# Four fused layers on one core: later weights converted later, base bias by tiles, output bias by accumulating transfers

## The chip, the cores and the metric

The kernel runs on one core of one Trainium2 chip. The metric is the device time in microseconds. TensorE multiplies, VectorE (DVE), ScalarE (ACT) and GpSimd (POOL) do elementwise work, and transfers are issued from the queues of SyncE (SP), GpSimd and, once, ScalarE. The engines run their own instruction lists in order and meet only in semaphores.

## The reference

Input x has 64 x 32 rows of 512 numbers, 2048 tokens in all, and there is a condition vector of 128 numbers for each of the 64 batches. Four layers follow one another, each with a residual:

```python
x = x + L0_ffn(L0_cond(x, cond))   # silu(c Wg^T) * (c Wu^T) Wd^T, width 1792
x = x + L1_ffn(L1_cond(x, cond))   # c W_base^T + b_base + top-2 of 8 LoRA experts of rank 16
x = x + L2_ffn(L2_cond(x, cond))   # c * sum(top-8 softmax of 64) + weights @ expert_bias
x = x + L3_ffn(L3_cond(x, cond))   # (c * in_scale) @ sign(W)^T * out_scale + bias
```

The conditioning step `cond` of layers 0, 2 and 3 mixes the 32 rows of a batch with a 32 x 32 matrix that a small network makes from the condition vector, and adds a bias; that of layer 1 is a grouped convolution over the 512 numbers with a bias. All is float32.

## The kernel before

The residual x lies in SBUF as `x_all`, 16 tiles of 128 tokens by 512. The work goes layer by layer, and in a layer over four groups `g` of four tiles (`GT` = 4, `G` = 4). Nothing is scheduled by a planner: each engine's list is written by hand, and the order in a list is the order in which it runs.

Layer 0 runs 14 slices of the feed-forward width for each group: gate and up products, silu on ScalarE, the product `hff` on VectorE, its high part on ScalarE and its low part `h_lo` on VectorE, and then the down product. `residual` (VectorE) adds the product to `x_all`. GpSimd's `part(g)` copies the new x of a group into a staging tile `prod`, which SyncE's `put_back(g)` writes to the DRAM scratch `y_dram`; SyncE's `regroup(g)` reads it back, shifted for the convolution, as 16 transfers into `stg`.

Layer 1, for each group: TensorE's `conv` makes the conditioned input from `stg`; VectorE's `cond1` turns it and adds `bias_bc` into `cT`; TensorE's `lora_a_router` makes the LoRA and router products, and `base` the base product of 32 matrix instructions. Meanwhile `route1` on VectorE shifts the logits, ScalarE takes their exponential (`exp`), and VectorE picks the two experts and writes `hm`. TensorE then runs the convolution of the next group, turns `hm`, and after ScalarE's copy `hmT` closes with `lora_b`. Base bias `bbase` is added to `x_all` by GpSimd's `base_bias(g)`, one instruction over four tiles, and VectorE's residual of the group waits for it (`s_base_bias`).

Between layers 0 and 1 ScalarE waits for the eight loads of the weights of layers 2 and 3 (`s_weights23`) and converts four of them: `eb_hi`, `in_w`, `out_w` and the signs `sgn` (`s_w_hi`). Only after these come its four exponentials. GpSimd makes the low halves of these weights after `base_bias(0)` and before `base_bias(1)`. SyncE issues the eight loads after `regroup(1)` and `bias(1, 1)`, and `put_back(3)` after them.

Layer 2 mixes with `cond`, routes with `route2`, and GpSimd's `add_scaled` adds the scaled input to `x_all`; VectorE's `final2` adds the rest (`s_x_new[2]`). In the last `layer2` TensorE runs `router3(0)`, waits for all of `s_x_new[2]`, and then for the chunks `FIRST3` of the mixing of group 1, with `turn_logits3(0)` after the first of them; `route3(0)` on VectorE needs that and follows `final2(3)` in VectorE's list.

Layer 3: ScalarE makes high halves (`high`) and copies the output scale (`out_scale`), VectorE and GpSimd make low halves, TensorE runs `sign_product`, VectorE rescales into `t1` (`s_rescaled`), GpSimd's `finish_3(g)` adds `t1` to `x_all`, and SyncE stores the tile. The output bias is added by GpSimd's `bias_3(g)`, four instructions, once the mixing has read the group.

Of the kernel before, what the change touches and what calls it, by code (L numbers as in the profile page):

```python
# [21 lines left out]
P = 128  # L22
D = 512
# [29 lines left out]
def build(nc, A, out):  # L53
    ctx = ExitStack()
    with ctx:
        def sb(name, shape, dt=F32):
            return ctx.enter_context(nc.sbuf_tensor(name, shape, dt))

        def sem(name):
            return ctx.enter_context(nc.semaphore(name))  # L60
# [82 lines left out]
        rb2 = sb("rb2", [P, E2])  # L143
        eb2 = sb("eb2", [P, D])
        wsg = sb("wsg", [P, S, D])
        bias3 = sb("bias3", [P, D])
        inc3 = sb("inc3", [P, D])
        outc3 = sb("outc3", [P, D])
        rcat = sb("rcat", [P, GT, P])
# [122 lines left out]
        s_scaled_hi = sem("s_scaled_hi")  # L272
        s_scaled_lo_even = sem("s_scaled_lo_even")
        s_scaled_lo_odd = sem("s_scaled_lo_odd")
        s_bias3 = sem("s_bias3")
        s_rescaled = sem("s_rescaled")
        s_tail = sem("s_tail")
        s_out = sem("s_out")
# [14 lines left out]
        def _(sp):  # L293
# [72 lines left out]
                sp.dma_start(dst[:], A[src]).then_inc(s_weights1, 16)  # L366
            regroup(1)
            bias(1, 1)
            sp.wait_ge(s_up, G * M)
            for dst, src in ((eb2, "eb2"), (inc3, "inc3"), (outc3, "outc3"), (wsg, "wsg"),  # L370
                             (wr2, "wr2"), (rb2, "rb2"), (wr3, "wr3"), (bias3, "bias3")):
                sp.dma_start(dst[:], A[src]).then_inc(s_weights23, 16)
            put_back(G - 1)
            for g in range(2, G):
                regroup(g)
                bias(1, g)
            for g in range(G):
                stage(g)
                bias(2, g)
# [12 lines left out]
        def _(pool):  # L392
# [73 lines left out]
            for g in range(1, G):  # L466
                block_diagonal(0, g)
                split_c(g)
                part(g - 1)
            block_diagonal(2, 0)  # L470
            part(G - 1)


            def base_bias(g):
                pool.wait_ge(s_weights1, LOADS1)
                xg = x_all[:, ds(g * GT, GT), :]
                pool.tensor_tensor(xg, xg, bbase[:].unsqueeze(1).broadcast_to([P, GT, D]),
                                   ALU.add).then_inc(s_base_bias, 1)

            pool.wait_ge(s_parted, NT)  # L480
            base_bias(0)
            pool.wait_ge(s_weights23, 16 * 8)
            pool.wait_ge(s_w_hi, 4)
            half = P // 2
            pool.wait_ge(s_base_bias, 1)
            pool.tensor_tensor(eb_lo[:], eb2[:], eb_hi[:].bitcast(F32), ALU.subtract).then_inc(s_w_lo, 1)
            pool.wait_ge(s_w_lo, 1)
            for n, (w, src) in enumerate(((in_w, inc3), (out_w, outc3))):
                pool.tensor_tensor(w[half:P], src[half:P], w[half:P].bitcast(F32), ALU.subtract).then_inc(s_w_lo, 1)
                pool.wait_ge(s_w_lo, n + 2)  # L490
            with pool.Fori(1, G) as g:
                base_bias(g)


            def add_scaled(g):
# [19 lines left out]

            def bias_3(g):
                pool.wait_ge(s_cond_mm[3], S * (g + 1))
                for j in range(g * GT, (g + 1) * GT):
                    pool.tensor_tensor(x_all[:, j, :], x_all[:, j, :], bias3[:], ALU.add).then_inc(s_bias3, 1)

            def finish_3(g, js):
                pool.wait_ge(s_bias3, GT * (g + 1))
                for j in js:
                    pool.wait_ge(s_rescaled, g * GT + j + 1)
                    xg = x_all[:, g * GT + j, :]
                    pool.tensor_tensor(xg, xg, t1[:, j], ALU.add).then_inc(s_x_new[3], 1)
# [19 lines left out]
        def _(pe):  # L546
# [155 lines left out]
            def layer1(g, more):  # L702
                base(g)
                pe.wait_ge(s_hm, g + 1)
                if more:
                    for q in range(Q - 1):
                        conv(g + 1, q)
                    pe.wait_ge(s_turned1, Q * (g + 1) + 1)
                    turn_hm(g)
                    conv(g + 1, Q - 1)  # L710
                    lora_b(g)
                    lora_a_router(g + 1)
                else:
                    cond(2, 0, SPARING, [nothing, nothing, nothing, lambda: (turn_hm(g), pe.wait_ge(s_cT[2], 1))])
                    lora_b(g)
                    pe.wait_ge(s_w_lo, 3)
                    pe.wait_ge(s_weights23, 16 * 8)
                    router2(0)
                pe.wait_ge(s_x_new[1], GT * (g + 1))


            def router2(g):
                pe.wait_ge(s_cT[2], S * (g + 1))
                for j in range(GT):
                    for s in range(S):
                        ins = mm(bank(4)[:, j * P:j * P + NPAD], cT[:, s, cols(j)], wr2[:, s], s == 0, s == S - 1)
                ins.then_inc(s_router2, 1)
# [7 lines left out]
            def layer2(g, more):  # L735
                for j in range(GT):
                    for s in range(S):
                        ins = pe.transpose(bank(j)[:, cols(s)], cT[:, s, cols(j)], ident)
                    ins.then_inc(s_c_back, 1)
                l, h = (2, g + 1) if more else (3, 0)  # L740
                cond(l, h, SPARING, [nothing, nothing, nothing,
                                      lambda: (turn_weights(g), pe.wait_ge(s_cT[l], S * h + 1))])
                pe.wait_ge(s_wT2, g + 1)
                for j in range(GT):
                    pe.wait_ge(s_t1, GT * g + j + 1)
                    mm(bank(j), wT[:, cols(j)], eb_hi[:], True, False)
                    mm(bank(j), wT[:, cols(j)], eb_lo[:], False, True).then_inc(s_product[2], 1)
                if more:
                    router2(g + 1)
                else:  # L750
                    pe.wait_ge(s_w_hi, 4)
                    router3(0)
                pe.wait_ge(s_x_new[2], GT * (g + 1))


            def router3(g):
# [91 lines left out]
        def _(act):  # L848
# [46 lines left out]
            layer0(G - 1, False)  # L895


            act.wait_ge(s_weights23, 16 * 8)
            act.wait_ge(s_product[0], G * GT)
            for dst, src in ((eb_hi, eb2), (in_w, inc3), (out_w, outc3)):  # L900
                copy(dst[:], src[:]).then_inc(s_w_hi, 1)
            act.activation(sgn[:], wsg[:], ACT.Sign).then_inc(s_w_hi, 1)

            def exp(s_ready, s_done, g, width):
                act.wait_ge(s_ready, g + 1)
                act.activation(ex[:, :, 0:width], lg[:, :, 0:width], ACT.Exp).then_inc(s_done, 1)

            with act.Fori(0, G) as g:
                exp(s_shifted1, s_exp1, g, E1)
                act.wait_ge(s_hm_turned, g + 1)  # L910
                copy(hmT[:], bank(4)).then_inc(s_hmT, 1)

            def scaled(g, j):
                act.wait_ge(s_c_back, GT * g + j + 1)
# [18 lines left out]
            for g in range(G):  # L933
# [11 lines left out]
                def out_scale(j):  # L945
                    act.wait_ge(s_out_scale, GT * g + j + 1)
                    copy(osc[:, j], bank(j)).then_inc(s_osc, 1)

                high(0)
                high(1)  # L950
                out_scale(0)
                high(2)
                high(3)
                for j in range(1, GT):
# [4 lines left out]
        def _(dve):  # L959
# [161 lines left out]
            with dve.Fori(0, G - 1) as g:  # L1121
                route1(g)
                cond1(g + 1)
                dve.wait_ge(s_base_bias, g + 1)
                residual(1, g)
            route1(G - 1)
            cond(2, 0, SPARING)
            dve.wait_ge(s_base_bias, G)
            residual(1, G - 1)


# [100 lines left out]
                    cond3(g + 1, [(s, UPPER[s]) for s in range(S)])  # L1232
            scale_out(G - 1, range(GT))

            dve.wait_ge(s_bias3, NT)
            dve.wait_ge(s_rescaled, NT)
            tt(x_all[:, NT - 1, D // 2:D], x_all[:, NT - 1, D // 2:D], t1[:, GT - 1, D // 2:D], ALU.add).then_inc(s_tail, 1)

# [89 lines left out]
```

## Time and profile before

| | |
|---|---|
| median of 3 runs (lowest, highest) | 588.41 us (588.16, 588.94) |
| the profiled execution | 588.53 us, of which the span is 586.3 us |
| busy: PE, PEld, DVE, ACT, POOL | 548.1, 420.5, 260.2, 133.9, 189.4 us |
| PE busy, tenths, slices of 14.7 us from 337.1 us | 9, 5, 2, 6, 9 |
| granted PE clock, tenths, same slices | 9, 8, 5, 8, 9 |
| chain that ended last | PE 80%, DVE 7%, issue 7%, DMA 2% |

"Busy" is the time in which an engine executed; PE is the matrix instruction itself and PEld its load of weights. The slices cut the span in 40. "Issue" in the chain is time in which an engine waited for nothing that the profile shows. A timeline row is: start in us, duration in us, engine, line, operation, target and sources, how many, and in brackets the idle time before with what ended it. Line 961 is a helper `tt` for VectorE, 548 the helper `mm` for TensorE and 850 the helper `copy` for ScalarE, so such rows are told apart by their tiles.

### The profile page before, as it was taken

Reading aid. Unit: us, or ns where it says so; the run is one execution under the profiler, and the core shown is the slowest. Engines: PE = TensorE matmul, PEld = TensorE weight load, DVE = VectorE, ACT = ScalarE, POOL = GpSimd, SP = SyncE. Lnnn points to the kernel's source line nnn. Section 1 sums busy time; section 2 is a strip of 40 time slices with the busy share of each in tenths; the row PEclk is TensorE's granted clock in tenths of the full one; section 3 lists DMA queues with packets and bytes.
Section 4 is the critical chain, followed back from the end, with each engine's and each line's share of the span. In section 5 each row is a group of like instructions: output and inputs, shape, how many; then the busy total and the mean of one; then the engine's idle time right before and its main releaser. Section 6 shows DMA issues by size and latency. Waiting matters only on the chain.

```text
span 586.3 us, 7216 instructions
## 1 busy us (share of the span) xinstructions
PE 548.1 (93%) x2689; PEld 420.5 (72%) x2689; DVE 260.2 (44%) x529; ACT 133.9 (23%) x230; POOL 189.4 (32%) x164
## 2 busy tenths in 40 slices
PE   7999999999999999999999995269999999989996
PEld 5788888888888888888888752035545589966884
DVE  4532245422227222253222340492526277887775
ACT  5322223222223222232222200310101022224332
POOL 2699981200004000012000000870000025478986
PEclk9999999999999999999999998589999999999999
DMA  8498130590001300003140099193681035111312
GB/s 298 152 421 305 29 91 0 123 181 0 0 0 55 106 0 0 0 1 89 27 101 1 0 121 237 48 120 41 81 151 18 14 111 137 28 19 18 126 70 111
DMA packets 84211, 50.32 MB, mean 86 GB/s; under 512 B 69600, under 2 KB 74464, under 8 KB 83424
## 3 DMA queue, kind: packets, MB, share of 16 engines
q1 hardware_dynamic: 82096, 38.97, 30.3%
q0 software_dynamic: 2016, 11.01, 5.2%
q8 instruction: 12, 0.20, 0.2%
q10 hardware_dynamic: 80, 0.08, 0.0%
q14 instruction: 7, 0.06, 0.0%
HBM read 31.93 MB, written 8.62 MB: 69 GB/s over the span
## 4 chain that ended last, share of the span: by engine, by line
PE 80%; DVE 7%; issue 7%; DMA 2%; POOL 1%; ACT 1%; SPq 0%; DVEq 0%; POOLq 0%
PE ps L548 80%; DMA xs<-in_x 2%; DVE cT L961 1%; POOL x_all L500 1%; DVE xs L961 1%; DVE c_lo L961 1%; DVE rest L1143 1%; DVE lg L961 1%; DVE t L961 0%; DVE c_lo_odd L961 0%; ACT c_hi L850 0%; DVE m L1139 0%; PE ps L732 0%; DVE rest L961 0%; PE ps L694 0%
## 5 line engine op out<-in xcount | busy, mean ns | idle before, releaser
L548 PE MATMUL ps<-c_lo,wl 128*128 128x512 f32 x448 | 173.0, 390 | 0.3 <-POOL c_lo L421 0.3
L548 PE MATMUL ps<-c_hi,wl 128*128 128x512 f32 x448 | 173.1, 390 | 0.2
L961 DVE TENSOR_TENSOR hff<-silu,ps 128x512 f32<-128x512 f32 x56 | 38.5, 688 | 164.5 <-PE ps L548 164.4
L548 PEld LDWEIGHTS ps<-c_lo,wl 128*128 128x128 f32 x448 | 84.1, 188 | 18.7 <-POOL c_lo L421 0.7
L548 PEld LDWEIGHTS ps<-c_hi,wl 128*128 128x128 f32 x448 | 84.1, 188 | 18.1 <-ACT c_hi L850 0.8
L548 PE MATMUL ps<-wl,h_hi 128*128 128x512 f32 x224 | 87.6, 391 | 0.0
L548 PE MATMUL ps<-wl,h_lo 128*128 128x512 f32 x224 | 87.2, 389 | 0.0
L961 DVE TENSOR_TENSOR h_lo<-hff,h_hi 128x512 fp32r<-128x512 f32 x56 | 44.8, 799 | 39.1 <-ACT h_hi L850 39.1
L421 POOL TENSOR_TENSOR c_lo<-cT,c_hi 128x512 fp32r<-128x512 f32 x8 | 10.7, 1342 | 157.7 <-ACT c_hi L850 157.7
L850 ACT ACTIVATE h_hi<-hff 128x512 fp32r<-128x512 f32 x56 | 35.4, 632 | 112.5 <-DVE hff L961 112.5
L884 ACT ACTIVATE silu<-ps 128x512 f32<-128x512 f32 x56 | 33.5, 598 | 116.4 <-PE ps L548 116.4
L548 PE MATMUL ps<-wbase,cT 128*128 128x512 f32 x128 | 55.6, 592 | 0.0
L548 PEld LDWEIGHTS ps<-wl,h_hi 128*128 128x128 f32 x224 | 42.0, 188 | 10.4 <-issue 1.7
L548 PEld LDWEIGHTS ps<-wl,h_lo 128*128 128x128 f32 x224 | 42.1, 188 | 8.5
L463 POOL COPY prod<-x_all 128x512 f32<-128x512 f32 x16 | 10.0, 642 | 111.7 <-DVE x_all L961 84.8
L548 PEld LDWEIGHTS ps<-wbase,cT 128*128 128x128 f32 x128 | 24.0, 190 | 28.7 <-issue 28.7
L548 PE MATMUL ps<-stg,wconv 128*64 128x512 f32 x64 | 18.6, 706 | 17.4 <-DVE hm L961 17.4
L961 DVE TENSOR_TENSOR cT<-ps,bias_bc 128x512 f32<-128x512 f32 x40 | 26.3, 686 | 19.2 <-PE ps L548 18.8
L433 POOL TENSOR_TENSOR blk<-agg,pack_c 128x512 f32<-128x512 f32 x9 | 9.4, 1041 | 75.7 <-PE ps L548 75.7
L548 PEld LDWEIGHTS ps<-blk,xs 128*128 128x128 f32 x256 | 31.3, 199 | 3.1 <-DMA xs<-in_x 1.9
L548 PE MATMUL ps<-blk,xs 128*128 128x128 f32 x256 | 32.4, 284 | 0.3 <-DMA xs<-in_x 0.3
L500 POOL TENSOR_TENSOR x_all<-x_all,t 128x512 f32 (+1 forms) x16 | 20.0, 1283 | 28.7 <-ACT t L915 28.7
(163 smaller groups left out, 649.9 us busy)
## 6 DMA issues: line engine op xcount, KB each, us to landing
wl<-in_wl POOLq DMA_DIRECT2D x14, 768.0 KB, 10.1
stg<-y_dram SPq DMA_DIRECT2D x64, 128.0 KB, 5.1
xs<-in_x SPq DMA_DIRECT2D x4, 1024.0 KB, 8.1
x_all<-in_x SPq DMA_DIRECT2D x1, 4096.0 KB, 14.7
y_dram<-prod SPq DMA_DIRECT2D x16, 256.0 KB, 2.2
xs<-x_all SPq DMA_DIRECT2D x4, 1024.0 KB, 4.9
out_x<-x_all SPq DMA_DIRECT2D x16, 256.0 KB, 2.0
bias_bc<-bias_dram SPq DMA_DIRECT2D x15, 256.0 KB, 5.3
```

The lines of the kernel that those rows point to most:

```text
L421: pool.tensor_tensor(c_lo[:, s], cT[:, s], c_hi[:, s].bitcast(F32), ALU.subtract).then_inc(s_c_lo_even, 1)
L433: pool.tensor_tensor(dst[:].rearrange("p j (b o) -> p j b o", b=TB), agg[:, COND[l], ds(g * GT, GT)].unsqueeze(2).broadcast_to([P, GT, TB, ...
L463: pool.tensor_copy(halves_x[:, j % 2], x_all[:, j, :].rearrange("p (s c h) -> p h s c", s=S, h=2)).then_inc(s_parted, 1)
L500: pool.tensor_tensor(xg, xg, t1[:, j:j + 1, :], ALU.add).then_inc(s_t1_added, 1)
L548: return pe.matmul(o, l, r, start=start, stop=stop)
L850: return act.activation(o, i, ACT.Copy)
L884: act.activation(silu[:, m % 2], bank(4 + 2 * (m % 2)), ACT.Silu).then_inc(s_silu, 1)
L961: return dve.tensor_tensor(o, a, b, op)
L1143: ins = dve.match_replace(rest[:, j], m8[:, j], logit[:, j], LOWEST)
```

## The change

On SyncE, `put_back(3)`, `regroup(2)` and `bias(1, 2)` go ahead of the loads of the later weights, which are seven, since `bias3` has no tile in SBUF any more; `regroup(3)` stays behind them. On ScalarE, the four conversions move from ahead of the exponentials into group 2, behind its `hmT` copy, and the loop over the groups is written out. On GpSimd, the base bias is added tile by tile, for groups 0 to 2 ahead of `part(3)` and for group 3 ahead of the low halves. On TensorE, the last `layer2` no longer waits for all of `s_x_new[2]`. On ScalarE, `out_scale(0)` of group 0 of layer 3 goes ahead of `high(0)`. On GpSimd, `bias_3(g)` issues one transfer that adds the bias from DRAM to the four tiles, with a semaphore for each group.

```diff
@@ SyncE
             regroup(1)
             bias(1, 1)
+            put_back(G - 1)
+            regroup(2)
+            bias(1, 2)
             sp.wait_ge(s_up, G * M)
             for dst, src in ((eb2, "eb2"), (inc3, "inc3"), (outc3, "outc3"), (wsg, "wsg"),
-                             (wr2, "wr2"), (rb2, "rb2"), (wr3, "wr3"), (bias3, "bias3")):
+                             (wr2, "wr2"), (rb2, "rb2"), (wr3, "wr3")):
                 sp.dma_start(dst[:], A[src]).then_inc(s_weights23, 16)
-            put_back(G - 1)
-            for g in range(2, G):
-                regroup(g)
-                bias(1, g)
+            regroup(3)
+            bias(1, 3)
@@ GpSimd
+            def base_bias(g):
+                for j in range(g * GT, (g + 1) * GT):
+                    pool.tensor_tensor(x_all[:, j, :], x_all[:, j, :], bbase[:], ALU.add).then_inc(s_base_bias, 1)
+
+            pool.wait_ge(s_weights1, LOADS1)
+            pool.wait_ge(s_parted, NT - GT)
+            for g in range(G - 1):
+                base_bias(g)
             block_diagonal(2, 0)
             part(G - 1)
...
             pool.wait_ge(s_parted, NT)
-            base_bias(0)
-            pool.wait_ge(s_weights23, 16 * 8)
+            base_bias(G - 1)
+            pool.wait_ge(s_weights23, 16 * 7)
             pool.wait_ge(s_w_hi, 4)
...
-            with pool.Fori(1, G) as g:
-                base_bias(g)
...
             def bias_3(g):
                 pool.wait_ge(s_cond_mm[3], S * (g + 1))
-                for j in range(g * GT, (g + 1) * GT):
-                    pool.tensor_tensor(x_all[:, j, :], x_all[:, j, :], bias3[:], ALU.add).then_inc(s_bias3, 1)
+                pool.dma_start(x_all[:, g * GT:(g + 1) * GT, :], A["bias3"].unsqueeze(1).broadcast_to([P, GT, D]),
+                               accum_op=ALU.add).then_inc(s_bias3[g], 16)

             def finish_3(g, js):
-                pool.wait_ge(s_bias3, GT * (g + 1))
+                pool.wait_ge(s_bias3[g], 16)
@@ TensorE, layer2
                 if more:
                     router2(g + 1)
+                    pe.wait_ge(s_x_new[2], GT * (g + 1))
                 else:
                     pe.wait_ge(s_w_hi, 4)
                     router3(0)
-                pe.wait_ge(s_x_new[2], GT * (g + 1))
@@ ScalarE
-            act.wait_ge(s_weights23, 16 * 8)
-            act.wait_ge(s_product[0], G * GT)
-            for dst, src in ((eb_hi, eb2), (in_w, inc3), (out_w, outc3)):
-                copy(dst[:], src[:]).then_inc(s_w_hi, 1)
-            act.activation(sgn[:], wsg[:], ACT.Sign).then_inc(s_w_hi, 1)
...
-            with act.Fori(0, G) as g:
+            for g in range(G):
                 exp(s_shifted1, s_exp1, g, E1)
                 act.wait_ge(s_hm_turned, g + 1)
                 copy(hmT[:], bank(4)).then_inc(s_hmT, 1)
+                if g == 2:
+                    act.wait_ge(s_weights23, 16 * 7)
+                    act.wait_ge(s_product[0], G * GT)
+                    for dst, src in ((eb_hi, eb2), (in_w, inc3), (out_w, outc3)):
+                        copy(dst[:], src[:]).then_inc(s_w_hi, 1)
+                    act.activation(sgn[:], wsg[:], ACT.Sign).then_inc(s_w_hi, 1)
...
+                if g == 0:
+                    out_scale(0)
                 high(0)
                 high(1)
-                out_scale(0)
+                if g > 0:
+                    out_scale(0)
```

VectorE's waits on `s_base_bias` count tiles, and its last wait on the output bias is for `s_bias3[3]`.

## Rows read from the trace of the kernel before

**Rows 1.** The page: the span.

```profile
span 586.3 us, 7216 instructions
```

**Rows 2.** The chain of waits, 340 to 416 us: start, us, what.

```profile
346.37 25.20 issue
```

**Rows 3.** Timeline of TensorE, 335 to 480 us.

```profile
345.75 13.90 PE L548 MATMUL ps<-wbase,cT 128*128 128x512 f32 x32
377.05 5.39 PE L548 MATMUL ps<-stg,wconv 128*64 128x512 f32 x12 [17.41 <-DVE hm L961]
...
415.75 1.12 PE L548 MATMUL ps<-stg,wconv 128*64 128x512 f32 x4
```

**Rows 4.** Timeline of ScalarE, 325 to 400 us.

```profile
366.52 0.63 ACT L850 ACTIVATE eb_hi<-eb 128x512 fp32r<-128x512 f32 x1 [31.10 <-DMA bias<-in_bias]
...
370.00 1.28 ACT L906 ACT_TABLE_LOAD   x1
```

**Rows 5.** Timeline of SyncE's queue, 325 to 475 us: the duration is that of issuing.

```profile
339.98 11.90 SPq L319 DMA_DIRECT2D stg<-y_dram  x16
...
352.67 3.37 SPq L372 DMA_DIRECT2D eb<-in_eb  x1
...
360.50 8.45 SPq L327 DMA_DIRECT2D y_dram<-prod  x4
```

**Rows 6.** Stages: length; PE, PEld, DVE, ACT, POOL busy (count); PEclk, DMA share, GB/s.

```profile
377.00:412.30 35.30, 29.80 (x92) 14.54 (x92) 18.66 (x35) 2.11 (x3) 14.66 (x4) 0.87 0.54 67
412.30:437.90 25.60, 25.60 (x95) 12.63 (x94) 10.75 (x35) 2.11 (x3) 0.00 (x0) 1.00 0.87 133
...
548.50:581.90 33.40, 32.65 (x210) 25.04 (x210) 22.37 (x45) 10.96 (x22) 28.89 (x22) 1.00 0.34 117
```

**Rows 7.** Timeline of VectorE, 335 to 415 us.

```profile
337.29 1.25 DVE L961 TENSOR_TENSOR cT<-tr,bias_bc 128x512 f32<-128x512 f32 x2
...
381.41 6.26 DVE L961 TENSOR_TENSOR cT<-tr,bias_bc 128x512 f32<-128x512 f32 x2
...
398.92 0.19 DVE L961 TENSOR_TENSOR lg<-ps,stat 128x32 f32<-128x32 f32 x1
...
401.76 0.69 DVE L961 TENSOR_TENSOR hm<-ps,lg 128x512 f32<-128x512 f32 x1
```

**Rows 8.** Timeline of GpSimd, 325 to 400 us.

```profile
344.27 1.22 POOL L463 COPY prod<-x_all 128x512 f32<-128x512 f32 x2 [73.94 <-DVE x_all L961]
...
377.68 14.34 POOL L477 TENSOR_TENSOR x_all<-x_all,bbase 128x2048 f32 x3 [0.37 <-POOL out_w L489]
```

**Rows 9.** Timelines of VectorE and of TensorE in layer 0, 290 to 297 us.

```profile
290.54 0.69 DVE L961 TENSOR_TENSOR hff<-silu,ps 128x512 f32<-128x512 f32 x1 [3.36 <-PE ps L548]
291.93 0.69 DVE L961 TENSOR_TENSOR h_lo<-hff,h_hi 128x512 fp32r<-128x512 f32 x1 [0.70 <-ACT h_hi L850]
...
295.71 0.39 PE L548 MATMUL ps<-wl,h_hi 128*128 128x512 f32 x1
```

**Rows 10.** Timeline of VectorE, 505 to 586 us.

```profile
521.50 0.75 DVE L1161 SCALAR_TENSOR_TENSOR x_all<-ps,stat,x_all 128x512 f32<-128x512 f32 x1 [0.48 <-POOL x_all L500]
523.61 0.19 DVE L1180 TENSOR_REDUCE stat<-ps 128x4 f32<-128x32 f32 x1 [1.36 <-PE ps L766]
```

**Rows 11.** Timeline of GpSimd, 505 to 586 us.

```profile
532.37 5.48 POOL L519 TENSOR_TENSOR x_all<-x_all,bias 128x512 f32<-128x512 f32 x4
...
562.13 5.02 POOL L519 TENSOR_TENSOR x_all<-x_all,bias 128x512 f32<-128x512 f32 x4
...
577.44 1.29 POOL L526 TENSOR_TENSOR x_all<-x_all,t 128x512 f32<-128x512 f32 x1 [0.28 <-DVE t L961]
```

**Rows 12.** GpSimd's loads of `wl` (durations in ns), and the page's transfers of `stg`.

```profile
L398 POOL DMA_DIRECT2D wl<-in_wl x14: 541/592/719, 4.6 to 28.0; - x14
...
DMA to landing us min/median/max: 4.5/10.1/18.1
...
stg<-y_dram SPq DMA_DIRECT2D x64, 128.0 KB, 5.1
```

More of the change, by code:

```diff
@@ L145, in build @@
         wsg = sb("wsg", [P, S, D])
-        bias3 = sb("bias3", [P, D])
         inc3 = sb("inc3", [P, D])
@@ L274, in build @@
         s_scaled_lo_odd = sem("s_scaled_lo_odd")
-        s_bias3 = sem("s_bias3")
+        s_bias3 = [sem(f"s_bias3_{g}") for g in range(G)]
         s_rescaled = sem("s_rescaled")
@@ L469, in _ @@
                 part(g - 1)
+            def base_bias(g):
[5 more added lines that the diff above has]
+                base_bias(g)
             block_diagonal(2, 0)
             part(G - 1)
[L474 to L478, printed above, removed]
             pool.wait_ge(s_parted, NT)
-            base_bias(0)
-            pool.wait_ge(s_weights23, 16 * 8)
+            base_bias(G - 1)
+            pool.wait_ge(s_weights23, 16 * 7)
             pool.wait_ge(s_w_hi, 4)
             half = P // 2
-            pool.wait_ge(s_base_bias, 1)
+            pool.wait_ge(s_base_bias, NT)
             pool.tensor_tensor(eb_lo[:], eb2[:], eb_hi[:].bitcast(F32), ALU.subtract).then_inc(s_w_lo, 1)
@@ L716, in layer1 @@
                     pe.wait_ge(s_w_lo, 3)
-                    pe.wait_ge(s_weights23, 16 * 8)
+                    pe.wait_ge(s_weights23, 16 * 7)
                     router2(0)
@@ L1123, in _ @@
                 cond1(g + 1)
-                dve.wait_ge(s_base_bias, g + 1)
+                dve.wait_ge(s_base_bias, GT * (g + 1))
                 residual(1, g)
@@ L1127, in _ @@
             cond(2, 0, SPARING)
-            dve.wait_ge(s_base_bias, G)
+            dve.wait_ge(s_base_bias, NT)
             residual(1, G - 1)
@@ L1233, in _ @@
             scale_out(G - 1, range(GT))
-            dve.wait_ge(s_bias3, NT)
+            dve.wait_ge(s_bias3[G - 1], 16)
             dve.wait_ge(s_rescaled, NT)
```

## The prediction

> **What bounds the kernel now.** I read the page's slices first (in the table above): TensorE is at nine tenths nearly everywhere, so only its holes can give anything. The one deep hole begins at 352 us. The profiled execution took 588.53 us, of which its span is 586.3 [rows 1]; the median of three runs is 588.41, so 0.1 us lower.
>
> The chain of waits names the hole. VectorE has the shifted router logits of group 0 of layer 1 ready at 346.4 and then stands for 25.20 us [rows 2]. In the timeline of TensorE the base product of group 0 runs from 345.75 to 359.6, and then comes nothing but an idle 17.41 us before the convolution of group 1 [rows 3]. ScalarE shows why: `eb_hi`, the first of four conversions of weights for layers 2 and 3, waits 31.10 us for the last load of the weights, and the exponential that VectorE needs is queued behind these four: it starts after its table load, 370.00 + 1.28 [rows 4]. The loads stand in SyncE's queue behind `regroup(1)`: 16 issues from 339.98 on, 11.90 us, then the eight loads from 352.67, then `put_back(3)` from 360.50 [rows 5].
>
> The hole has a tail. From 377.0 to 412.3 TensorE is busy 29.80 of 35.30 us at a granted clock of 0.87; the next, undisturbed round of the same work takes 25.60 us, all busy, at 1.00 [rows 6]. The 9.7 us of difference are 5.5 idle and 4.2 slow clock. The idle is VectorE's: two bias additions into `cT` take 6.26 us where the same pair takes 1.25 elsewhere [rows 7], and beside them GpSimd runs three base-bias additions of 2048 elements, 14.34 us together, 4.78 each [rows 8]. So a VectorE addition of two SBUF operands stood until one such GpSimd instruction ended.
>
> The Trainium skill, "SBUF — State Buffer", on contention, says the same: VectorE with two SBUF inputs and a GpSimd instruction that reads SBUF exclude each other for the whole instruction. By that rule an instruction cut to a quarter costs each VectorE addition at most a quarter of that wait.
>
> **The change part by part.**
>
> *The conversions behind exponential 2 (ScalarE), loads behind `regroup(2)` (SyncE).* Exponential 0 starts at about 346.6, its table loaded before. In an undisturbed round `hm` is written 3.5 us after the shift (398.92 to 402.45) [rows 7], so it is there at about 350, before the base product ends at 359.6. What is late next is `regroup(1)`: its last issue is at 351.9 [rows 5], and such a transfer takes 5.1 us to land [rows 12], so the data are there at about 357, before 359.6. Should they come later, each us costs one. The idle 17.41 us goes whole: -17.4. With no idle stretch ahead of it, the round of 35.3 us becomes one of 25.6: -9.7 more.
>
> SyncE's queue: `put_back(3)` now issues from 352.67. Its four issues, with the two copies of GpSimd between them, take 8.45 us now [rows 5], so GpSimd ends `part` at about 361 and `regroup(2)` waits for nothing but the convolution of group 1, done at about 364. It takes 11.9 us of issue [rows 5] and 5.1 to land, 17.0; the data are wanted 21.0 us after that convolution (its last part ends at 416.87 in the next round, which begins again at 412.3 + 25.6 [rows 3, 6]): no cost. The seven loads then issue from about 377. Now they take 366.5 - 352.7 = 13.8 us from the first issue to the conversion that waits for them [rows 4, 5], so they are there at about 391. ScalarE comes to them behind the transposed `hm` of group 2, at about 414: 23 us of cover, and `regroup(3)` cannot start before about 390 anyhow. The four conversions take 3.6 us (366.52 to the table load at 370.00 [rows 4]); the exponential of group 3 may come late by a few us without cost, because the base product of 13.9 us [rows 3] hides it. If that cover were gone it would cost 3.6 us.
>
> *Base bias by tiles.* Twelve additions (groups 0 to 2) move into layer 0, after the loads of `bbase`, which issue at the sixth slice of the last group, about 290.5 [rows 9]. GpSimd is idle there: its next row waits 73.94 us [rows 8]. Twelve at 1.28 us (that is 5.02 / 4 of an equal addition [rows 11]) make 15.4 us; even if those loads take 13.8 us, as the eight of layers 2 and 3 do, they end by 320. Beside them `h_lo` ends at 292.6 and its product is issued at 295.71, a slack of 3.1 us [rows 9], against one wait of 1.28, or 2.6 if both VectorE instructions of a slice wait: 0. The last four run at about 361 to 366, beside the first additions into `cT` of group 1. Bounds: 0, if the two miss each other; 2.6, if both additions of the first pair wait a whole instruction. I take +0.5, near the lower end, since an addition hits an instruction in mid-run and the additions are not the last thing TensorE waits for in an undisturbed round.
>
> *The wait dropped in the last `layer2`.* TensorE waits for all of group 3's new x, which ends at 522.25, though the first chunk of the mixing of group 1 reads only group 1 and writes a bank that is free. `turn_logits3` is queued behind this chunk, and VectorE starts `route3` at 523.61 [rows 10]. With the wait gone, chunk and transposition run while VectorE finishes; VectorE, whose order is unchanged, starts at 522.3. TensorE's own queue moves up as much. -1.3 us. The most it could fail by is all of it.
>
> *`out_scale(0)` first for group 0.* ScalarE's five copies keep their sum (0.63 us each [rows 4]), and the product waits for the last of the high halves, which stays where it is. 0, between -0.6 and +0.6.
>
> *The output bias by transfers.* GpSimd loses four additions of 5.0 us in each group [rows 11] and gets an issue instead: one of its issues takes 0.59 us [rows 12], and up to 5.0 it would cost no more than now. TensorE is busy 32.65 of the last 33.40 us before its end [rows 6], so GpSimd's freed time is worth 0 to 0.5; I take 0. What is new is that `finish_3(g)` waits for the landing. The tightest is the last: issued where the additions begin, 562.13, wanted by the first closing addition of group 3, 577.44 [rows 11]: 15.3 us. No accumulating transfer is in the trace. The nearest: loads of 768 KB from the same queue, 14 of them and most in each other's way, take 4.5 to 18.1, median 10.1 [rows 12]. Below 15.3 the cost is 0; at 18.1 it is 2.8. I take 10.1, the value of the same queue, so 0.
>
> The Trainium skill, "DMA: Bandwidth & Descriptors", on the software path, fits 2.0 us plus bytes over 436 GB/s, which would be an estimated 4.4 us for this size and no cost either; it has no figure for accumulating, and no row here shows one.
>
> **Sum.** 588.53 - 17.4 - 9.7 + 0.5 - 1.3 = 560.6.
>
> **The rivals.**
>
> *The transfers land late, but gain remains.* An accumulating transfer reads its target too, so it may be slower than the rows of plain loads. Between 15.3 and 20 us each us of landing adds one at the end, and above that up to two: 25 us give about 570. For it: no row shows this operation. Against it: the transfer queues are nearly empty in this stretch.
>
> *Slower than before: the same transfers as a chain.* `bias_3(3)` is issued after `finish_3(1)`, which waits for the landing of `bias_3(1)`, issued where its additions now start, 532.37 [rows 11]. With a landing time L the span is 532.4 + L + some 5 for the closing additions + L + 8.9 (from 577.44 to the end) - 27.8 for what is gained ahead = 518.5 + 2L. It decides from L = 34 us; at 40 it gives a span of 598.5, a time of about 601. That is twice the slowest landing seen.
>
> *The stall only moves.* Weights landing later than the end of ScalarE's `hmT` copy of group 2 would hold exponential 3. It takes over 23 us of delay before it starts to cost; or contention in layer 0 or round 1 is larger than the rows say (each VectorE instruction waits for more than one of the tile additions). Then the tail of 9.7 is not won: up to 570.
>
> **How the numbers follow.** Forecast 0.88: 560.6, own range 558.7 to 565.8. The low end takes away the 0.5 of contention, 0.5 for the freed GpSimd and 0.6 plus rounding for `out_scale`; the high end adds 2.1 of contention, 2.8 for landing and 0.3. Late landing with gain 0.06, tail not won 0.04, slower than before 0.02. A measurement of this kernel tells about 0.2% (1.2 us) from no change. Faster 0.97, same 0.01, slower 0.02. The range is the forecast's own.
>
> **What would show it.** Right: no idle TensorE between base product and convolution in the first round of layer 1, granted clock 1.00 there, rounds of 25.6 to 26.5 us; twelve base-bias rows on GpSimd between 295 and 320; `route3` of group 0 starting 0.1 us after the last new x; accumulating transfers landing in under 15 us. Wrong: an idle of VectorE or TensorE at `finish_3`, `hm` of group 0 later than 359 us, a `cT` addition in round 1 of over 2 us, or a slice of layer 0 longer than at present.

## The result and the profile after

The changed kernel takes 561.52 us (559.42 to 561.84, four runs) against 588.67 us (588.16 to 589.56, four runs): a ratio of 0.953, 95% interval 0.9503 to 0.9556. The profiled execution took 561.39 us, its span 559.6.

The page: span, busy slices of TensorE, granted clock.

```profile
span 559.6 us, 7186 instructions
PE   7999999999999999999999999999999999989996
PEclk9999999999999999999999999999999999999999
```

The hole is gone, and the granted clock is at nine tenths or more in every slice. The answer to [rows 3] is this timeline of TensorE: the base product ends where the convolution begins, and the router product of the next group waits for nothing.

```profile
346.96 13.90 PE L546 MATMUL ps<-wbase,cT 128*128 128x512 f32 x32
360.79 2.91 PE L546 MATMUL ps<-stg,wconv 128*64 128x512 f32 x12
...
368.84 3.97 PE L546 MATMUL ps<-war,cT 128*128 128x136 f32 x32
372.65 13.90 PE L546 MATMUL ps<-wbase,cT 128*128 128x512 f32 x32
386.47 2.91 PE L546 MATMUL ps<-stg,wconv 128*64 128x512 f32 x12
```

The exponential of group 0, which stood behind the conversions in [rows 4], now follows VectorE's shift at once:

```profile
347.61 0.23 ACT L898 ACTIVATE ex<-lg 128x32 f32<-128x32 f32 x1 [9.68 <-DVE lg L962]
```

GpSimd's timeline, against [rows 8]: twelve base-bias tiles run in layer 0, four beside the first round of layer 1.

```profile
301.54 16.49 POOL L472 TENSOR_TENSOR x_all<-x_all,bbase 128x512 f32<-128x512 f32 x12 [31.05 <-DMA wlb<-in_wlb]
...
360.43 5.40 POOL L472 TENSOR_TENSOR x_all<-x_all,bbase 128x512 f32<-128x512 f32 x4
```

VectorE's additions into `cT` in that round, against the 6.26 us of [rows 7]: 2.89 for the pair that meets GpSimd, 1.24 for the other.

```profile
363.49 2.89 DVE L962 TENSOR_TENSOR cT<-tr,bias_bc 128x512 f32<-128x512 f32 x2
...
367.54 1.24 DVE L962 TENSOR_TENSOR cT<-tr,bias_bc 128x512 f32<-128x512 f32 x2
```

**The ledger by stages.** TensorE's timeline repeats so exactly that starts of the same instruction cut the span into stages that can be compared between kernels (us). Each column is a difference of two starts: S0, from 0 to the router product of group 0; A, to the convolution of group 1; B, to that of group 2 (round 1); C, to that of group 3; D, to the last transposition of layer 2's weights; E, to the first mixing chunk of `FIRST3`; F, to `in_scales(0)`; H, to `router3(1)`; I, to the end of the span.

| kernel | S0 | A | B | C | D | E | F | H | I |
|---|---|---|---|---|---|---|---|---|---|
| before | 341.96 | 35.09 | 35.27 | 25.55 | 78.05 | 6.38 | 5.08 | 6.06 | 52.86 |
| changed | 343.18 | 17.61 | 25.68 | 25.55 | 78.03 | 5.03 | 5.07 | 6.66 | 52.79 |
| difference | +1.22 | -17.48 | -9.59 | 0 | 0 | -1.35 | 0 | +0.60 | -0.07 |

From the start of the router product on, the changed kernel is 27.92 us shorter. S0 is 1.22 us longer, and the chain of waits puts that into the first 20 us, ahead of everything that was changed: the load of the first x, and the small matrix instructions behind it. Changed kernel first, then the kernel before:

```profile
2.13 12.58 DMA xs<-in_x
...
14.75 4.65 PE ps L546 x20
```

```profile
2.13 12.12 DMA xs<-in_x
...
14.29 3.95 PE ps L548 x20
```

Over all runs below S0 lies anywhere from 340.77 to 343.18 us, with no order by kernel. So the medians scatter by some 2 us through the start alone, and where a few tenths matter I read the stages.

The 20 small instructions belong to the 32 of the first mixing. These in the changed kernel, then in e10 below, where S0 is 340.78:

```profile
14.75 5.99 PE L546 MATMUL ps<-blk,xs 128*128 128x128 f32 x32 [0.61 <-DMA xs<-in_x]
```

```profile
14.12 4.16 PE L545 MATMUL ps<-blk,xs 128*128 128x128 f32 x32
```

Within the 32, one starts every 0.21 us up to 19.3 us in the changed kernel, 17.4 in the one before and 15.0 in e10, and every 0.11 us from there on. In all fourteen profiles S0 less the end of these 32 is 322.3 to 322.5 us. So the scatter of S0 is the 0.8 us between their earliest and latest start and, for the larger part, the moment at which their rate doubles. The halved spacing fits TensorE's two clock levels of 1.2 and 2.4 GHz, but the profile gives a granted clock of 1.00 for this stretch, so the clock is inferred here, and no run shows why the moment differs.

### The profile page after: what moved, and what is told of

Same layout as the page of the kernel before. It is cut to its first block, busy times and chain, and to the rows that moved or that the text cites. A ratio compares the mean times of both kernels' runs of the same rounds, so it can differ in the third digit from the quotient of the medians.

```text
span 559.6 us, 7186 instructions
## 1 busy us (share of the span) xinstructions
PE 545.0 (97%) x2689; PEld 419.3 (75%) x2689; DVE 251.9 (45%) x529; ACT 129.9 (23%) x227; POOL 177.7 (32%) x164
## 4 chain that ended last, share of the span: by engine, by line
PE 91%; DVE 5%; DMA 2%; issue 1%; ACT 1%; SPq 0%; DVEq 0%
PE ps L546 89%; DMA xs<-in_x 2%; DVE c_lo L962 1%; DVE cT L962 1%; DVE t L962 0%; DVE rest L1144 0%; PE ps L692 0%; PE ps L730 0%; PE ps L786 0%; PE ps L736 0%; DVE wcat L962 0%; DVE c_lo_odd L962 0%; DVE m L1140 0%; DVE lg L962 0%; DVE rest L962 0%
## 5 line engine op out<-in xcount | busy, mean ns | idle before, releaser
L472 POOL TENSOR_TENSOR x_all<-x_all,bbase 128x512 f32<-128x512 f32 x16 | 21.9, 1403 | 31.1 <-DMA wlb<-in_wlb 31.1
L463 POOL COPY prod<-x_all 128x512 f32<-128x512 f32 x16 | 10.1, 644 | 54.8 <-DVE x_all L962 37.3
L1013 DVE STREAM_TRANSPOSE tr<-ps 128x512 f32<-128x512 f32 x16 | 11.2, 708 | 34.3 <-PE ps L546 34.3
```

The costliest lines, as they stand in the source:

```text
L463: pool.tensor_copy(halves_x[:, j % 2], x_all[:, j, :].rearrange("p (s c h) -> p h s c", s=S, h=2)).then_inc(s_parted, 1)
L472: pool.tensor_tensor(x_all[:, j, :], x_all[:, j, :], bbase[:], ALU.add).then_inc(s_base_bias, 1)
L1013: dve.transpose(tr[:, q % 2], bank(4 + q)).then_inc(s_turned1, 1)
```

## The experiments

**e1: the conversions alone.** The kernel before with this edit only:

```diff
-            act.wait_ge(s_weights23, 16 * 8)
-            act.wait_ge(s_product[0], G * GT)
-            for dst, src in ((eb_hi, eb2), (in_w, inc3), (out_w, outc3)):
-                copy(dst[:], src[:]).then_inc(s_w_hi, 1)
-            act.activation(sgn[:], wsg[:], ACT.Sign).then_inc(s_w_hi, 1)
...
-            with act.Fori(0, G) as g:
+            for g in range(G):
                 exp(s_shifted1, s_exp1, g, E1)
                 act.wait_ge(s_hm_turned, g + 1)
                 copy(hmT[:], bank(4)).then_inc(s_hmT, 1)
+                if g == 0:
+                    act.wait_ge(s_weights23, 16 * 8)
+                    act.wait_ge(s_product[0], G * GT)
+                    for dst, src in ((eb_hi, eb2), (in_w, inc3), (out_w, outc3)):
+                        copy(dst[:], src[:]).then_inc(s_w_hi, 1)
+                    act.activation(sgn[:], wsg[:], ACT.Sign).then_inc(s_w_hi, 1)
```

> The kernel before, with one edit: the four conversions move behind the hmT copy of group 0 (with group 2 the low halves on GpSimd would wait for ever, since base_bias(1) is queued behind them). My theory: the idle 17.4 us between base product and convolution goes, but put_back(3) still stands behind the eight loads, so base_bias(0) ends only at about 373, the residual of group 0 waits for it, and TensorE idles about 6 us in round 1: 588.5 - 17.4 - (9.7 - 7.5) = about 569 us (566 to 572). Rival (the conversions are the whole of it, the moves on SyncE and GpSimd are worth nothing): 561.5 us. Rival (the 9.7 us of tail is lost in full whatever ScalarE does): 571 us and a round 1 of over 35 us.

Measured: 568.17 us (567.79 to 569.77), ratio 0.9656 [0.9638, 0.9674]. Stage A is 17.61 us, as in the changed kernel, and B 31.86. TensorE's base product of group 1, and VectorE's residual of group 0 that released it:

```profile
375.88 15.67 PE L548 MATMUL ps<-wbase,cT 128*128 128x512 f32 x32 [4.17 <-DVE x_all L961]
```

```profile
372.89 2.48 DVE L961 TENSOR_TENSOR x_all<-x_all,ps 128x512 f32 x4 [6.58 <-POOL x_all L477]
```

The idle stretch belongs to ScalarE's order alone. What stays is the late base bias: VectorE stands 6.58 us for it, TensorE 4.17, and its clock falls to 0.89 in the 15.7 us behind. My theory stands.

**e2, e3, e4: size and place of the base bias.** In the changed kernel, e2 and e3 put all of it behind `part(3)`:

```diff
-            pool.wait_ge(s_weights1, LOADS1)
-            pool.wait_ge(s_parted, NT - GT)
-            for g in range(G - 1):
-                base_bias(g)
             block_diagonal(2, 0)
             part(G - 1)
+            pool.wait_ge(s_weights1, LOADS1)
             pool.wait_ge(s_parted, NT)
-            base_bias(G - 1)
+            for g in range(G):
+                base_bias(g)
```

e2 and e4 make it one instruction over four tiles, with the waits counted in groups:

```diff
-                for j in range(g * GT, (g + 1) * GT):
-                    pool.tensor_tensor(x_all[:, j, :], x_all[:, j, :], bbase[:], ALU.add).then_inc(s_base_bias, 1)
+                xg = x_all[:, g * GT:(g + 1) * GT, :]
+                pool.tensor_tensor(xg, xg, bbase[:].unsqueeze(1).broadcast_to([P, GT, D]),
+                                   ALU.add).then_inc(s_base_bias, 1)
```

> The changed kernel, with all four base-bias additions behind part(3), as before, and each one instruction over four tiles, as before. My theory: they run from about 360 to 380 beside the additions into cT of round 1; each of these waits for the end of one instruction of 4.8 us, so the pairs take 5 to 6 us again instead of 2.9 and 1.2 and TensorE idles 6 to 9 us: 567 to 571 us. Rival (the tail came from the cold clock behind the idle stretch, not from GpSimd): 561.5 us, since the idle stretch is gone here too.

> The changed kernel, with the sixteen base-bias additions by tiles, all behind part(3). My theory: the additions into cT wait for one instruction of 1.3 us each, 5 us in all less about 1.5 us of slack: 2.5 to 4 us over the changed kernel, 564 to 565.5 us. Rival (the size of the instruction doesn't matter, only the total of 20 us beside VectorE): the same time as with the coarse ones there. Rival (only the size matters, the place is worth nothing): 561.5 us.

> The changed kernel, with the base bias in its new places, but one instruction over four tiles. My theory: three instructions of 4.8 us beside layer 0, where the slack of h_lo is 3.1 us: each can hold a down product by up to 1.7 us, and the one of group 3 holds the first addition into cT by about 1.7 us: 0.5 to 5 us over the changed kernel, 562 to 566.5 us. Rival (layer 0 hides everything, whatever the size): 561.5 us, within 0.5.

Measured: e2 573.0 us (572.8 to 574.55), e3 562.17 (561.49 to 562.65), e4 559.79 (559.73 to 561.62). Stage B: 38.60, 28.28 and 25.55 us, against 25.68 in the changed kernel and 25.55 in an undisturbed round.

VectorE in e2, then TensorE in e2:

```profile
361.99 6.95 DVE L961 TENSOR_TENSOR cT<-tr,bias_bc 128x512 f32<-128x512 f32 x2
...
370.10 8.65 DVE L961 TENSOR_TENSOR cT<-tr,bias_bc 128x512 f32<-128x512 f32 x2
```

```profile
378.80 5.43 PE L545 MATMUL ps<-war,cT 128*128 128x136 f32 x32 [11.34 <-DVE cT L961]
```

VectorE in e3, then TensorE in e3:

```profile
361.98 3.31 DVE L960 TENSOR_TENSOR cT<-tr,bias_bc 128x512 f32<-128x512 f32 x2
...
366.44 3.42 DVE L960 TENSOR_TENSOR cT<-tr,bias_bc 128x512 f32<-128x512 f32 x2
```

```profile
369.92 3.97 PE L544 MATMUL ps<-war,cT 128*128 128x136 f32 x32 [2.46 <-DVE cT L960]
```

One VectorE addition loses up to one GpSimd instruction: 15.60 us for four additions beside instructions of 4.8 us, 6.73 beside those of 1.3, and 2.5 alone. e2 lies outside what I expected: I took the waits to be no more than in the kernel before. There the additions began beside the first of three instructions, the pair of [rows 7] lost 5.0 us and the next pair 3.1, and TensorE stood 5.5 us in the round [rows 6]. Here four instructions followed without a gap and TensorE stood 11.34 us; the granted clock was 0.76 over the 15 us up to 378.8 and 0.71 over the 5.2 us behind, so the router product took 5.43 us for 3.87.

The rival that put the whole tail down to the idle stretch ahead is out: there was none, and the tail was longer than ever. But a part of the tail is the idle stretch's, which I had not separated. Two stretches of the kernel before, in the columns of [rows 6], with the granted clock third from the end:

```profile
377.00:382.40 5.40, 5.35 (x13) 1.29 (x13) 2.34 (x3) 0.00 (x0) 5.03 (x3) 0.50 0.00 0
393.20:398.50 5.30, 5.27 (x33) 5.27 (x34) 2.37 (x4) 0.00 (x0) 0.00 (x0) 0.71 1.44 160
```

The first is the convolution right behind the 17.41 us of idle: at 0.50 it took 5.39 us [rows 3], and in e2, with no idle stretch ahead, 2.91. That, and 0.1 us in the transposition behind it, makes 2.6 us of the 9.7. The second is the router product behind VectorE's stall, 5.42 us for 3.87: with the 5.5 us of idle, some 7 us are GpSimd's.

e3 in its stage is 2.6 us over the changed kernel, as expected, though its median shows 0.7 of it, since its S0 was 1.5 us shorter.

e4 shows what I had not worked out: three instructions of 4.8 us beside layer 0 cost nothing. S0 alone could not show it, since it scatters by more. But behind the first 25 us the chain of waits is one run of 1449 matrix instructions up to the router product: 318.57 us in e4, 318.49 in e3, where nothing lies beside layer 0, 318.63 in the changed kernel and 318.56 in the one before. The timeline of GpSimd in e4:

```profile
300.43 14.69 POOL L472 TENSOR_TENSOR x_all<-x_all,bbase 128x2048 f32<-128x2048 f32 x3 [31.38 <-DMA wlb<-in_wlb]
```

So the place is what gains; the cut into tiles gains nothing in its new place. Whether some other timing of these three would hold a down product was not tried.

**e5: output bias by GpSimd's instructions.** The changed kernel with the old `bias_3` and `bias3` as an eighth load.

```diff
-                pool.dma_start(x_all[:, g * GT:(g + 1) * GT, :], A["bias3"].unsqueeze(1).broadcast_to([P, GT, D]),
-                               accum_op=ALU.add).then_inc(s_bias3[g], 16)
+                for j in range(g * GT, (g + 1) * GT):
+                    pool.tensor_tensor(x_all[:, j, :], x_all[:, j, :], bias3[:], ALU.add).then_inc(s_bias3[g], 1)
```

> The changed kernel, with the output bias added by GpSimd's instructions again (bias3 loaded as an eighth weight). My theory: the transfers land in 9.4 us where 15.3 are free, and GpSimd's time is not on the path, so neither form costs anything: 561.5 us, within 0.7, and the layer 3 stretch of the same length within 0.3. Rival (GpSimd's freed time is worth something): 562 to 563 us.

Measured: 560.06 us (558.13 to 561.66). Its stages from the router product to the end add up to 216.45 us, those of the changed kernel to 216.42; stage I is 52.94 against 52.79. That 0.15 us is too little to tell from one profile of each. My theory stands; the median is lower by the start (S0 341.95).

**e6: the wait back.**

```diff
                 if more:
                     router2(g + 1)
-                    pe.wait_ge(s_x_new[2], GT * (g + 1))
                 else:
                     pe.wait_ge(s_w_hi, 4)
                     router3(0)
+                pe.wait_ge(s_x_new[2], GT * (g + 1))
```

> The changed kernel, with TensorE's wait for all of the new x of group 3 back behind router3(0). My theory: route3(0) starts 1.3 us behind the last new x again: 562.8 us (562.4 to 563.2). Rival (the product of group 0 waits for the low halves anyway and the gain is lost there): 561.5 us.

Measured: 562.11 us (560.32 to 563.38); stage E 6.40 us against 5.03, all other stages within 0.05. The wait is worth 1.37 us and no other stage takes it back.

```profile
494.29 1.16 PE L546 MATMUL ps<-prod,x_all 128*128 128x128 f32 x8 [1.30 <-DVE x_all L1162]
```

**e7: the output scale behind the high halves.**

```diff
-                if g == 0:
-                    out_scale(0)
                 high(0)
                 high(1)
-                if g > 0:
-                    out_scale(0)
+                out_scale(0)
```

> The changed kernel, with out_scale(0) of group 0 behind high(0) and high(1) again. In the changed kernel the stretch from scale_in to the first rescaled product grew from 5.0 to 5.6 us, with VectorE's two low halves at 3.05 us where they took 2.3, so the early output scale holds the high halves 0.5 us and makes the low halves of VectorE and GpSimd collide. My theory: 560.9 us, 0.4 to 0.7 under the changed kernel. Rival (the collision comes from GpSimd's missing bias additions): 561.5 us with the same 5.6 us.

Measured: 559.47 us (558.92 to 561.45); stage H 6.07 us against 6.66. VectorE's low halves of group 0 in e7, and the chain of waits of the changed kernel over the same stretch:

```profile
501.31 0.86 DVE L959 TENSOR_TENSOR c_lo<-cT,c_hi 128x512 fp32r<-128x512 f32 x1
502.42 1.44 DVE L959 TENSOR_TENSOR c_lo<-cT,c_hi 128x512 fp32r<-128x512 f32 x1 [0.25 <-ACT c_hi L848]
```

```profile
501.61 0.60 ACT osc L848
502.21 1.05 ACT c_hi L848 x2
503.25 0.02 issue
503.28 3.06 DVE c_lo L962 x2
506.34 0.04 issue
506.38 2.63 PE ps L546 x37
```

The early copy costs 0.59 us, and e5 rules out the rival: with GpSimd's bias additions back, H was 6.65. What e7 gave back elsewhere is stage B, 26.23 us against 25.68: the four base-bias tiles met VectorE's additions at a worse moment. From the router product to the end e7 takes 216.33 us against 216.42, so nearly all of the 2.05 us between the medians is the start (S0 340.77). e1 and the kernel before, with their own order, have H at 6.06.

**e8, e9: landing made longer.** The changed kernel with one (e8) or two (e9) more accumulating transfers of 1 MB into a spare tile ahead of each bias transfer; each group's extra transfers wait for those of the group before. GpSimd also clears the spare tile once, behind the base bias.

```diff
+                pool.dma_start(spare[:], A["bias3"].unsqueeze(1).broadcast_to([P, GT, D]),
+                               accum_op=ALU.add).then_inc(s_spare, 16)
                 pool.dma_start(x_all[:, g * GT:(g + 1) * GT, :], A["bias3"].unsqueeze(1).broadcast_to([P, GT, D]),
                                accum_op=ALU.add).then_inc(s_bias3[g], 16)
```

> The changed kernel, with one more accumulating transfer of 1 MB into a spare tile issued ahead of each bias transfer on the same queue. The bias transfers landed in 9.1 to 9.7 us where 15.3 are free. My theory: landing of 15 to 18.8 us and so 0 to 3.5 us at the end: 561 to 565 us. Rival (queued transfers don't delay each other): landing under 11 us, 561.5 us. Rival (the issue itself, 1.3 us each on GpSimd, is what counts): 562.8 us and more with landing unchanged.

> The same with two more transfers ahead of each. My theory: landing of 21 to 28 us, which is beyond the 15.3 us free, so finish_3 waits and the end moves by 6 to 13 us: 567 to 575 us, with GpSimd idle ahead of its closing additions. Rival (there is more room than 15.3 us, since VectorE and TensorE need finish_3 only one group later): under 564 us.

Measured: e8 564.19 us (564.02 to 564.36, two runs), e9 580.14 (both runs). GpSimd's transfers into `x_all` in the changed kernel, in e8 and in e9 (least, median, most):

```profile
DMA to landing us min/median/max: 9.1/9.4/9.7
```

```profile
DMA to landing us min/median/max: 13.7/15.4/17.8
```

```profile
DMA to landing us min/median/max: 17.8/21.9/25.4
```

In e8 the time is as expected and the reason is another. `finish_3` waited 0.7 us in all, ahead of group 0. What ended last was SyncE's 256 KB load of the mixing bias of group 3, which VectorE needs for `cond3(3)`; the waits, and the chain:

```profile
DVE xs L972 <- DMA bias_bc<-bias_dram: 2.6, 1, 2.6
POOL x_all L534 <- DMA x_all<-in_bias: 0.7, 1, 0.7
```

```profile
520.17 15.08 DMA bias_bc<-bias_dram
```

Stage I grew by 4.2 us: TensorE stood 2.6 us for VectorE there, and the granted clock was 0.76 over the 7.2 us behind. The slowest such load takes 6.8 us in the kernel before, 9.3 in the changed one and 15.1 in e8, and where GpSimd adds the bias itself 5.9 (e5) and 6.8 (e12): the bias transfers of GpSimd's queue slow the small load of SyncE's. Both rivals of e8 are out, since landing did grow.

e9 came out far above its range, 19.5 us of it in stage I. This is no clean test: GpSimd stood 13.4 us for the experiment's own order between spare transfers.

```profile
POOL x_all L535 <- DMA x_all<-in_bias: 14.0, 3, 9.8
POOL spare L525 <- DMA spare<-in_bias: 13.4, 3, 4.6
```

The rival with more room is out all the same. The last bias transfer was issued at 547.30, and `finish_3(3)` stood for it at the very end of the chain:

```profile
571.24 3.94 POOL L535 TENSOR_TENSOR x_all<-x_all,t 128x512 f32<-128x512 f32 x3 [9.75 <-DMA x_all<-in_bias]
```

That is 23.9 us of landing, of which 14.2 were covered, near the 15.3 I had worked out. The 25.4 us are those of group 2.

**e10: SyncE's order as before.**

```diff
             bias(1, 1)
-            put_back(G - 1)
-            regroup(2)
-            bias(1, 2)
             sp.wait_ge(s_up, G * M)
...
-            regroup(3)
-            bias(1, 3)
+            put_back(G - 1)
+            for g in range(2, G):
+                regroup(g)
+                bias(1, g)
```

> The changed kernel, with SyncE's order as before: the seven loads ahead of put_back(3) and regroup(2). My theory: put_back(3) ends about 8 us later, regroup(2) is issued from about 371 and has landed at about 388 where TensorE wants it at 386.5: 0.5 to 2 us, 562 to 563.5 us. Rival (the loads' place is what removed the stall): 570 us or more. Rival (no cost, there is cover): 561.5 us.

Measured: 559.64 us (559.15 to 560.12); stage B 25.54 us. My theory falls and so does the rival that made the loads' place the cause: it costs nothing. SyncE's queue, and TensorE's convolution of group 2:

```profile
357.86 8.92 SPq L326 DMA_DIRECT2D y_dram<-prod  x4
366.89 10.85 SPq L318 DMA_DIRECT2D stg<-y_dram  x16
```

```profile
383.93 2.91 PE L545 MATMUL ps<-stg,wconv 128*64 128x512 f32 x12
```

`regroup(2)` begins at 366.9, 4 us earlier than I had put it, and is issued by 377.7. With the median landing of 5.1 us it is there at an estimated 382.8, 1.1 us ahead of its use. GpSimd's last four tiles moved behind VectorE's additions, so round 1 is even 0.14 us shorter.

**e11: the best of both.** The changed kernel with e7's and e4's edits.

> The changed kernel, with out_scale(0) of group 0 behind the high halves again and the base bias in its new places as one instruction for four tiles. The runs so far give 0.6 us for the first (the stretch from in_scales to router3(1) was 6.07 us against 6.66) and 0.1 us for the second (round 1 of 25.55 us against 25.68). My theory: 0.7 us under the changed kernel, 560.8 us, and both stretches as short as in the single runs. Rival (the two meet elsewhere): 561.5 us.

Measured: 558.86 us (558.1 to 559.22), ratio 0.948 [0.9466, 0.9495]. Stage H is 6.07, B 25.67; from the router product to the end 215.79 us against 216.42. Of the 2.7 us between the medians 0.6 are the edits, the rest is the start (S0 341.11). The 0.1 us of e4 did not come back: one instruction of 4.5 us met the first additions at another moment (pair of 2.87 us).

**e12: three edits alone.** The kernel before with the conversions behind group 2, the base bias by tiles in its new places and the dropped wait; all else as before.

> The kernel before with three of the edits alone: the conversions behind group 2, the base bias by tiles in its new places, and the dropped wait. SyncE's order, the output bias by GpSimd's instructions and the place of out_scale(0) are those of before. My theory: these three are the whole gain. Round 1 of 25.54 us as in the run with the loads ahead, 6.07 us from in_scales to router3(1) as in the run with out_scale behind, so 0.6 to 0.7 us under the changed kernel: 560.8 us or less, within 0.4% of it. Rival (the loads ahead and the additions on GpSimd meet and cost something together): 562 us and more, with a longer round 1 or a wait of TensorE in layer 3.

Measured: 560.05 us (559.55 to 560.25), ratio 0.9505 [0.9484, 0.9525]. The stages are 17.61, 25.55, 25.54, 78.02, 5.02, 5.07, 6.05 and 52.84: 215.70 us, the shortest of all fourteen profiles, and 28.6 under the kernel before. Three of the six edits are the whole gain.

| stage | before | e1 | e2 | e3 | e4 | e6 | e7 | e10 | e11 | e12 | changed |
|---|---|---|---|---|---|---|---|---|---|---|---|
| A | 35.09 | 17.61 | 17.61 | 17.61 | 17.61 | 17.61 | 17.61 | 17.61 | 17.60 | 17.61 | 17.61 |
| B | 35.27 | 31.86 | 38.60 | 28.28 | 25.55 | 25.63 | 26.23 | 25.54 | 25.67 | 25.55 | 25.68 |
| E | 6.38 | 6.41 | 5.03 | 5.03 | 5.03 | 6.40 | 5.04 | 5.02 | 5.03 | 5.02 | 5.03 |
| H | 6.06 | 6.06 | 6.66 | 6.67 | 6.66 | 6.66 | 6.07 | 6.66 | 6.07 | 6.05 | 6.66 |

## Why the prediction was right, term by term

The forecast of 560.6 us is 0.8 under the profiled execution of 561.39, and the changes come out as forecast in place and nearly in size. That the terms' 27.9 us meet the stages' 27.92 so closely is partly luck: contention came out 0.4 us cheaper than I took it, `out_scale(0)` 0.6 us dearer.

- *Idle stretch, -17.4.* Stage A: -17.48. e1 shows that ScalarE's order alone gives it. `regroup(1)` was in time, as worked out.
- *Tail, -9.7, with +0.5 for contention.* Stage B: -9.59, so contention cost 0.13. It was nearer to its lower end than I took it: one pair took 2.89 us instead of 1.25, but TensorE needs it only 1.5 us later. Three runs agree on these 1.5 us: the additions of the round lost 1.6 us here, 2.2 in e7 and 4.2 in e3, and the round grew by 0.13, 0.68 and 2.73. So the moment at which GpSimd's instructions meet them decides.
- *The cause of the tail.* I split it as 5.5 idle and 4.2 clock, and did not say whose the clock is. With no idle stretch ahead and GpSimd's instructions back, e2 has a tail with both parts. But of the 4.2 us 2.6 came from the idle stretch ahead, the convolution at a clock of 0.50, and only the rest from the stall that GpSimd caused. Both causes were removed, so the term was right as a whole.
- *Tiles.* I gave the gain to moving and cutting together. e4 shows that the cut is worth nothing once twelve tiles lie in layer 0; e3 shows that the cut alone would have left 2.6 us.
- *SyncE's order, 0.* Right for the changed kernel, but the edit is no condition of the gain either (e10). What I had not seen is that the old order has 1.1 us of cover.
- *Dropped wait, -1.3.* Stage E: -1.35; e6: 1.37.
- *`out_scale(0)` first, 0 within 0.6.* Stage H: +0.60, the upper bound. This is the step that failed, the point value and its reason. I argued that the product waits for the last high half, which stays where it is. It does, but behind it comes the last low half. The first two high halves moved 0.6 us later, GpSimd's two low halves then run without a gap, and VectorE's two, which exclude each other with them, take 3.05 us instead of 0.86 and 1.44 with a gap.
- *Output bias, 0.* Stage I: -0.07, e5 0.15. Landing was 9.4 us, close to the 10.1 I took, which is luck: that was the median of plain loads of another size, most of them in each other's way; an issue takes 1.3 us rather than 0.59, under the 5.0 it replaces. What the late-landing rival missed is another queue: at landings of 13.7 to 17.8 us (e8) `finish_3` hardly waited, but the load of `bias_bc` on SyncE's queue was late.
- *The start.* 1.2 us of S0 are in no term; no edit touches them, and they lie in the first mixing, as shown above.

The Trainium skill, "SBUF — State Buffer", on the pair of ports that VectorE and GpSimd share, says that the later one blocks for the whole instruction. e2 and e3 agree, with 3.3 and 1.1 us lost for each addition beside instructions of 4.8 and 1.3 us. The fit of the Trainium skill, "DMA: Bandwidth & Descriptors", on the software path, gave an estimated 4.4 us for a plain transfer of this size; the accumulating one took 9.4, and the measurement decides.

## What to carry to other kernels

When an engine stands for "issue", follow the queue of the engine that should release it: work of a later stage, parked at a stage boundary, held the first instruction of the next stage here, and moving it behind the first loop round (e1) gave 20.9 of the 27.9 us. Then look for what is late next, which here was another engine's long instruction excluding VectorE, and move that to a stage with slack before cutting it. Undo the parts one at a time: three of six edits carried everything, and one of the others cost 0.6 us.

## What the runs showed of the hardware that I had not expected

An accumulating transfer of 1 MB from DRAM, bias rows repeated four times, landed in 9.1 to 9.7 us alone and 15.4 behind another of its kind, so the second added 6.0; and such transfers slowed a 256 KB load of another queue, made of 128 B pieces, from at most 6.8 us to 9.3 and 15.1.

A TensorE stall of 11.34 us (e2) was followed by a router product of 5.43 us instead of 3.87, at a granted clock of 0.71, a mean over both levels of 1.2 and 2.4 GHz. One of 5.45 us (kernel before) cost the same, 5.42 us at 0.71. One of 2.46 us (e3) cost nothing that shows: 3.97 us, as in the changed kernel without a stall, at 1.00.

S0 varies by up to 2.4 us between kernels that are the same up to there but for GpSimd's base bias. Between the changed kernel and the one before, 1.15 of the 1.22 us lie in the first load of x (0.46) and the 20 small matrix instructions behind it (0.70). Over all profiles the moment at which the first mixing's instructions speed up lies anywhere from 15.0 to 19.4 us; why it differs stays open. The scatter is more than the dropped wait and the misplaced output scale are worth together.
